# Half of the int8 weight loads of a feed-forward stage issued from ScalarE's queue instead of SyncE's

## The reference

```python
x = x + _layernorm(attn(_layernorm(x), Wq, Wk, Wv, Wo))

# feed-forward: HIDDEN = 2048, INTER = 8192, x is (4, 4096, 2048) float32
def _qmatmul(x, w_int8, scale):
    return jnp.einsum('bsh,ho->bso', x, w_int8.astype(x.dtype)) * scale
gate = silu(_qmatmul(x, w_gate, s_gate))
up   = _qmatmul(x, w_up, s_up)
y    = _qmatmul(gate * up, w_down, s_down)

x = x + _layernorm(y)          # y of _layernorm(x)
```

## Time and profile before

| | us |
|---|---|
| timed runs, median of 2 | 9520.02 |
| timed runs, lowest and highest | 9481.81, 9558.24 |
| the profiled execution | 9306.34 |
| its span on core 3 (first to last instruction) | 9304.8 |
| spans of the eight cores | 9278.2 to 9304.8 |
| mean granted TensorE clock of the cores | 0.765 to 0.768 |

### The profile page before, as it was taken

How to read it: one execution, slowest core, us unless ns; L and a number is a source line. 1 busy time by engine, 2 the same in 40 slices (tenths; PEclk the granted TensorE clock), 3 DMA queues, 4 the chain that set the end, 5 groups by cost and what they waited for, 6 DMA issues and landing times.

```text
span 9304.8 us, 70507 instructions; the slowest of 8 cores (9278.2 to 9304.8 us)
## 1 busy us (share of the span) xinstructions
PE 5782.3 (62%) x22552; PEld 2288.9 (25%) x22552; DVE 3155.7 (34%) x3361; ACT 3928.4 (42%) x3640; POOL 618.5 (7%) x328
## 2 busy tenths in 40 slices
PE   2447999544444444436577873787737778367774
PEld 1223444211111111102233331333313333123331
DVE  3320000355555655552322223222232222232222
ACT  3334555566666666653322224232242222422224
POOL 0000000000000000000011111111111111111111
PEclk8779999756565665557788885888868888688886
DMA  2111223110100000013122221222212222112221
GB/s 83 68 66 60 71 79 97 44 28 14 28 25 16 25 16 25 16 51 117 64 66 68 66 68 50 61 68 68 68 52 57 68 66 70 57 52 65 67 73 52
DMA packets 524708, 524.77 MB, mean 56 GB/s; under 512 B 86080, under 2 KB 462912, under 8 KB 512064
## 3 DMA queue, kind: packets, MB, share of 16 engines
q1 hardware_dynamic: 471360, 444.74, 16.4%
q10 hardware_dynamic: 52992, 75.52, 2.2%
HBM read 444.69 MB, written 75.50 MB: 56 GB/s over the span
## 4 chain that ended last, share of the span: by engine, by line
PE 48%; ACT 20%; DVE 15%; issue 10%; DMA 5%; ACTq 1%; POOL 0%; DVEq 0%; SPq 0%; POOLq 0%
PE pw L1287 11%; PE pn L1287 11%; PE pw L339 7%; PE pw L421 5%; ACT p_exp L745 5%; PE pw L1390 4%; PE pn L1390 4%; DVE f_wb L1265 3%; ACT L745 3%; DVE p_sums L862 2%; ACT f_wdb L1376 2%; PE pw L1039 2%; DMA f_wd<-wd_t 2%; DVE f_raw L1413 1%; PE pw L713 1%
## 5 line engine op out<-in xcount | busy, mean ns | idle before, releaser
L1287 PE MATMUL pw<-f_ln2T,f_wb 128*128 128x512 bf16 x4096 | 1029.5, 416 | 310.4 <-DVE f_wb L1265 310.4
L1287 PE MATMUL pn<-f_ln2T,f_wb 128*128 128x512 bf16 x4096 | 1026.9, 415 | 233.1 <-DVE f_wb L1265 233.1
L1337 POOL TENSOR_TENSOR f_fuse<-f_gb,f_uf 128x512 bf16<-128x512 bf16 x256 | 512.4, 2004 | 7992.0 <-DVE f_uf L1323 6261.3
L1307 ACT ACT_TABLE_LOAD x128 | 164.2, 1283 | 1810.8 <-PE pw L1287 1621.5
L1265 DVE CAST f_wb<-f_w 128x4096 bf16<-128x4096 int8 x256 | 631.6, 2487 | 475.1 <-PE pw L1287 424.4
L1390 PE MATMUL pw<-f_fuse,f_wdb 128*128 128x512 bf16 x2048 | 614.4, 429 | 285.0 <-ACT f_wdb L1376 193.7
L745 ACT ACT_TABLE_LOAD x512 | 656.9, 1283 | 299.5 <-PE pw L718 106.8
L784 DVE TENSOR_TENSOR p_esum<-p_esum,p_exp 128x128 f32<-128x128 f32 (+15 forms) x512 | 661.8, 1293 | 93.6 <-DVE p_exp L759 47.0
L339 PE MATMUL pw<-xlnT,p_wb 128*128 128x512 bf16 x3072 | 667.1, 380 | 12.6 <-ACT p_ev L356 5.0
L1287 PEld LDWEIGHTS pw<-f_ln2T,f_wb 128*128 128x128 bf16 x4096 | 426.9, 105 | 902.3 <-issue 505.7
L1376 ACT ACT_TABLE_LOAD x256 | 328.4, 1283 | 754.8 <-PE pn L1390 385.2
(11 more groups left out here) (141 smaller groups left out, 5169.4 us busy)
## 6 DMA issues: line engine op xcount, KB each, us to landing
f_wd<-wd_t SPq DMA_DIRECT2D x256, 512.0 KB, 3.8
f_w<-wg_t SPq DMA_DIRECT2D x128, 512.0 KB, 5.0
f_w<-wu_t SPq DMA_DIRECT2D x128, 512.0 KB, 5.1
p_xt<-xkv SPq DMA_DIRECT2D x32, 1024.0 KB, 4.9
p_wf<-wv SPq DMA_DIRECT2D x64, 256.0 KB, 3.0
p_wf<-wk SPq DMA_DIRECT2D x32, 512.0 KB, 6.0
v_s<-p_ev ACTq DMA_DIRECT2D x128, 128.0 KB, 1.7
kt_s<-p_ev ACTq DMA_DIRECT2D x128, 128.0 KB, 1.9
```

The costliest lines, as they stand in the source:

```text
L1287: mm = t_.matmul(B[sub][:], fwb[pi][:, dc * 256 + sub * 128: dc * 256 + (sub + 1) * 128], ln2T[:, dc * 512:(dc + 1) * 512], start=(dc == 0 ...
L1337: gpool[il] = kb.inc(g.tensor_tensor(fuse[:, il * 512:(il + 1) * 512], fgb[il % 4][:], fuf[il % 2][:], ALU.mult), "ePOOL")
```

## The change

Two loads choose the program they are put in. The load of the up weights (phase 1) and the down load of every odd block are now issued by ACT. What they wait for, what they copy and which semaphores they raise is the same, and so are the order and content of all other programs.

```diff
@@ -1241,7 +1241,7 @@
                                                       in_=srcw[:, DC // 2:DC, :]),
                                        "qG%d" % (li % 2), 16)
                                 wld[li] = c["qG%d" % (li % 2)]
-                            block.sync(s_w2)
+                            (block.sync if phase == 0 else block.scalar)(s_w2)
 
                             for gpair in range(2):
                                 il0 = grp * 4 + gpair * 2
@@ -1359,7 +1359,7 @@
                                     out=fwd8[pp][:],
                                     in_=wd_t[:, icb0 * D:(icb0 + 2) * D]),
                                     "qD%d" % pp, 16)
-                            block.sync(s_wd)
+                            (block.sync if pp == 0 else block.scalar)(s_wd)
                             WDL = c["qD%d" % pp]
 
                             def a_wd(a, pr=pr, pp=pp, dg=dg, WDL=WDL):
```

## The result

The changed kernel takes 10247.96 us (median of 11 runs, 9982.67 to 10582.79), the kernel before 9546.86 us in the same series (10 runs). The ratio is 1.073, with a 95% interval of 1.070 to 1.076: slower by 7.3%. Forecast were 10210 us in 9990 to 10480, and slower by more than 2% with a chance of 0.95.

A forecast was written before the change was run, and what follows sets the result against it. PE and DVE in turn were taken to set the time, weights never late. Up loads 686 us plus down loads 6 us make 692 us; on the timed median 9520 that gives 10212, rounded to 10210 us, range 9990 to 10480.

The forecast's parts named there:

- The exposed load: Gate/up part: up load issued after phase 0's last Silu wait starts PE 8.6 us late per group, less in four groups.
- the point of decision: Up load: one leaving by 8.6 us before phase 0's end is hidden, a later one lies open.
- The clock: Gate/up matmuls: the step after each new gap runs at a lower granted clock, 2.2 us more.
- a longer gap costs no more: Gate/up steps: idle time beyond 3.39 us adds no clock loss; a step after 8.10 us idle took 8.57 us.
- The 2200 us: Sign in the profile after: L1287's busy time rises by about 140 us to 2200 us.
- The down part: Odd down loads on ACT: its program runs ahead of unfinished activations, so loads leave almost as early as on SP.
- The 6 us: Down part: later issue of the moved loads costs 0.2 us per run of eight, 6 us in all.
- I count that as nothing: Second run of eight down blocks: changed neighbours of the last down loads cost nothing, -1 to +1 us in 16 places.
- the landing times: One 512 KB load lands in 3.5 to 9.5 us, which moves the total by -115 to +270 us.
- ACT holding back its DMAs: Rival: ACT issues loads only after the activation before them finishes; about 10520 us, chance 0.08.
- The clock falling for the whole step: Rival: step after the new gap runs at 0.50 throughout, 13.8 us; 298 us more, about 10510 us, chance 0.07.
- No loss: Rival: ACT's program passes over waiting instructions, so up loads leave a group ahead; 9400 to 9530 us, chance 0.05.

The follow-up runs named there:

- up_early: Changed kernel with the up load, still issued by ACT, put ahead of its group's phase 0; undisturbed spans about 9305 us, 0.2% over before.
- sp_late: Kernel before, with SP issuing the up load only after phase 0's last matmul and no load from ACT; spans about 9897 us, 6.6% over before.
- up_mid: Changed kernel with the up load one step earlier, between the Silus of phase 0's two steps; ratio to before 1.018, spans about 9383 us.
- cast_first_after: Changed kernel with DVE's next cast put ahead of a phase 1 step's eviction and POOL's product; spans about 9355 us, 0.7% over before.
- serial_again: Changed kernel with ACT waiting for the up load's first half before issuing the second, run again for a second profile; ratio to before 1.083.
- down_only: Kernel before with only the odd down loads moved to ACT, up loads staying on SP; spans about 9329 us, 0.5% over before.
- down_held: down_only with SP holding the next quarter's gate load until the seventh down block's cast is done; spans about 9284 us.
- serial_halves: Changed kernel with ACT waiting for the up load's first half to land before issuing the second; 10234.01 us against 9442.03 before.

## Why the prediction was right

**The exposed load.** The step that the forecast rests on held: the load can't leave before the last Silu's wait has passed, and nothing covers it. Issue, landing and cast came out within 0.1 us of the working in the group shown (8.5 us late against 8.6). As a sum, PE idled 562 us more, where 8.6 us in 60 groups and 7.2 us in four gave 545. The working had left out that the last group of each quarter shares its transfer time with the first down load: there the cast came 7.1 us after the issue, in the others 5.8 (averages of core 6). up_early and sp_late show that this is the cause, and up_mid that the point of decision lies where it was put.

**The clock.** The mis-sized term: 2.2 us x 64 = 141 us forecast, 78 measured. The slow start of the new step measured 1.95 us. The 2.2 us came from a slip in the division: it took 6.91 us, the distance from start to start, for the steps without a gap, while the busy time has 7.07 us for each of them. With 7.07 it gives (4 x 8.03 - 2 x 7.07) / 2 = 8.99 us, 1.9 us more, which is 18 us less in 64 groups. The other 45 us are those that came back: the working left out that the steps after the old gaps don't keep their price. They had averaged 8.98 us by sorting and fell to 8.57. Where there are no such gaps, the full price shows (cast_first_after). That a longer gap costs no more held for 8.9 us, and not quite for 10.3 us (serial_again). The 2200 us named beforehand for L1287's busy time came out as 2134.2.

**The down part.** That ACT's program runs ahead of its activations held, in down_only and in the rows of its issues. The 6 us came out as 43 us alone and as 3 us on PE in the two profiles compared (15 us on core 5 of both); ACT's wait for f_wd<-wd_t did not stay near 69.7 us but rose to 91.1. The step that failed is "I count that as nothing": I looked at what SP no longer sends beside the last down loads, and not at the wait that left SP's program together with the eighth load. down_held shows that it was this wait. In the changed kernel the size is small; there the up loads had left SP's queue too.

**The sum and its level.** 692 us forecast, 656 measured on undisturbed dies and 642 between the profiled executions. The forecast for the median, 9520 + 692 = 10212, is 36 us below 10247.96, with a median of before that was itself 27 us higher in the longer series. That the two medians differ by 701 us, so close to 692, is in part luck: at an undisturbed clock the forecast was 36 us too high, by the clock's term above all. The range was wide enough; the landing times that made most of it were not needed.

**The rivals.** ACT holding back its DMAs: refuted by the issue at 6490.21, inside a_wd(2), and by down_only. The clock falling for the whole step: refuted, 9.0 us per step and not 13.8. No loss: refuted; the wait in front of the last Silu holds ACT's whole program, and the up loads leave 0.07 us after that Silu has started. The Trainium skill's account of the wait queue and the execution FIFO (Perfetto Trace Analysis, Per-instruction lifecycle) agrees on running ahead with the issue 0.62 us before the Silu's end; for waits that are instructions of their own, as here, these runs show that no load passed one.

## What to carry to other kernels

A DMA moved to a compute engine's queue inherits every wait that stands before it in that engine's program; what counts is not how busy the engine is but when its program reaches the place. Put a load ahead of the compute that the engine waits for, at least issue, landing and cast (8.5 us here) before it is wanted; then the engine that issued it hardly mattered here (19 us of 9286). Look also at the queue that the DMA leaves: its wait goes with it, and what was queued behind it now runs ahead and may get in front of the very transfer that was moved.

## What the runs showed of the hardware that I had not expected

- A gap of 3.39 us on PE slowed the next step in 93 of 96 cases before (core 3; 91 to 95 over the cores), and in 72 of 96 after the change (core 6; 58 to 76), though the gap was the same. In the one looked at closely, this was the 1.2 GHz level. Gaps of 2.8 us did it in 16 of 32 cases after the change (all cores), gaps above 8 us always (80 of 80 on each core). What decides between the cases these runs do not show.
- There are stretches at a granted clock of 0.82, neither of the two levels, in which 32 uninterrupted matmuls take 8.4 to 8.6 us instead of 7.07. They came in the profiled executions of several kernels here, up_mid, serial_halves and serial_again among them, on some cores and not on others.
- In down_only (core 0) a load issued behind 2 MB of another queue's loads, 0.8 us after the last of these was issued, let its cast's table load start 6.1 us after the issue, against 4.5 and 5.2 us for ACT's two loads before it in the same run of eight (issues at 6311.60 and 6319.35, table loads at 6316.05 and 6324.51).
